# Cross-attention stage: side work moved between VectorE, GpSimd and the end of the stage

## The reference, cut to what matters

```python
cq = heads(ci @ cq_w, NH, CHD)            # 16 heads of 16
ckv = encoder_outputs @ ckv_w
ck, cv = jnp.split(ckv, 2, axis=-1)
cctx = sdpa(cq, ck, cv, causal=False)     # 512 queries x 1601 keys
cctx = cctx.transpose(0, 2, 1, 3).reshape(b, l, CC)      # CC = 256
hidden_states = hidden_states + cctx @ cdense_w          # 256 x 512
mi = rms_norm(hidden_states, ln_post_attn_w)
v_out = jax.nn.silu(mi @ v_gate) * (mi @ v_up) @ v_down
l_out = jax.nn.silu(mi @ l_gate) * (mi @ l_up) @ l_down
hidden_states = hidden_states + jnp.where(vm, v_out, l_out)
```

## Time and profile before

| | us |
|---|---|
| median of 3 runs | 2831.53 (2830.54 to 2838.45) |
| the profiled execution, device time | 2844.54 |
| its span | 2842.7 |
| PE busy | 2294.1 (81% of the span) |
| DVE busy | 1615.3 (57%) |
| ACT busy | 937.5 (33%) |
| POOL busy | 363.3 (13%) |

### The profile page before, as it was taken

One profiled execution on the slowest core, in us unless ns is written; L12 is line 12 of the kernel. 1 busy time (PEld: TensorE's weight loads), 2 busy tenths in 40 slices (PEclk: granted clock), 3 DMA queues, 4 the chain that ended last, 5 costly groups with the idle time before them and its releaser, 6 DMA issues. The chain is left out here.

```text
span 2842.7 us, 35384 instructions
## 1 busy us (share of the span) xinstructions
PE 2294.1 (81%) x13534; PEld 1463.7 (51%) x13534; DVE 1615.3 (57%) x2444; ACT 937.5 (33%) x1627; POOL 363.3 (13%) x388
## 2 busy tenths in 40 slices
PE   6987858869659867768687488999999859999968
PEld 3663545745446634546444333333333327877856
DVE  4384533664442854336554388788887626676534
ACT  1131132222121312312212237767777742222101
POOL 0120002110002200011100001111111112221211
PEclk8986879977779867889777669999999979999989
DMA  4033053250261240431412634433344013333322
GB/s 147 27 85 83 16 140 103 64 130 2 68 174 31 75 104 13 110 136 53 110 31 68 120 79 99 83 60 61 65 70 97 14 42 82 105 98 105 105 80 71
DMA packets 194542, 227.90 MB, mean 80 GB/s; under 512 B 53942, under 2 KB 128058, under 8 KB 193066
## 3 DMA queue, kind: packets, MB, share of 16 engines
q1 hardware_dynamic: 187404, 217.97, 31.1%
q0 software_dynamic: 6656, 6.96, 1.0%
q10 hardware_dynamic: 288, 0.27, 0.0%
HBM read 162.76 MB, written 34.98 MB: 70 GB/s over the span
## 5 line engine op out<-in xcount | busy, mean ns | idle before, releaser
L1435 DVE TENSOR_REDUCE quarters<-ps 128x2 f32<-128x804 f32 x512 | 484.4, 989 | 76.5 <-PE ps L1469 76.1
L1388 ACT ACTIVATE pT_x<-ps 128x512 f32<-128x512 f32 (+1 forms) x832 | 451.5, 594 | 166.6 <-PE ps L1497 144.7
L1469 PE MATMUL ps<-kx_ring,qx_ring 63*128 63x402 f32 x1024 | 235.5, 476 | 72.8 <-DVE quarters L1435 36.8
L184 DVE TENSOR_TENSOR w_lo<-w_raw,w_hi 128x512 fp32r<-128x512 f32 (+2 forms) x357 | 278.4, 780 | 12.2
L182 DVE CAST w_hi<-w_raw 128x512 fp32r<-128x512 f32 (+2 forms) x357 | 177.0, 496 | 185.2 <-PE ps L190 109.0
L1512 PE MATMUL ps<-pT_x,vx_ring 128*17 128x256 f32 (+1 forms) x3328 | 268.9, 397 | 0.0
L1469 PEld LDWEIGHTS ps<-kx_ring,qx_ring 63*128 63x128 f32 x1024 | 101.2, 197 | 268.9 <-DVE quarters L1435 162.8
L877 ACT ACTIVATE pT_s<-ps 128x1024 f32<-128x1024 f32 (+3 forms) x128 | 88.8, 704 | 355.7 <-PE ps L963 355.7
L188 PE MATMUL ps<-mi_h,w_hi 128*128 128x512 f32 (+1 forms) x440 | 174.6, 397 | 37.9 <-issue 25.7
L894 DVE TENSOR_REDUCE row_max_s<-ps 128x1 f32<-128x128 f32 (+3 forms) x256 | 123.8, 490 | 136.0 <-PE ps L933 132.1
L1497 PE MATMUL ps<-qx_ring,kx_ring 64*128 64x512 f32 (+1 forms) x832 | 181.6, 433 | 21.9 <-ACT pT_x L1388 18.4
(11 more groups left out here) (273 smaller groups left out, 4430.3 us busy)
## 6 DMA issues: line engine op xcount, KB each, us to landing
kx_ring<-cross_k_by_part SPq DMA_DIRECT2D x96, 200.2 KB, 7.3
w_raw<-L_xattn_l_qkv SPq DMA_DIRECT2D x48, 256.0 KB, 2.9
w_raw<-L_xattn_v_qkv SPq DMA_DIRECT2D x48, 256.0 KB, 2.7
w_raw<-L_xattn_l_gate SPq DMA_DIRECT2D x40, 256.0 KB, 2.9
w_raw<-L_xattn_l_up SPq DMA_DIRECT2D x40, 256.0 KB, 2.8
w_raw<-L_xattn_l_down SPq DMA_DIRECT2D x40, 256.0 KB, 2.7
q_st<-early SPq DMA_DIRECT2D x32, 256.0 KB, 5.2
cross_v_by_group<-v_aug SPq DMA_DIRECT2D x16, 442.0 KB
```

The lines of the kernel that those rows point to most:

```text
L184: nc.vector.tensor_tensor(out=lo, in0=raw, in1=hi.bitcast(f32), op=ALU.subtract).then_inc(s_split, 1)
L1388: nc.scalar.activation(pT[0:kn, u % 3, j, :], ps[0:kn, 5 + v % 3, :], ACT.Exp, scale=SCALE)\
L1435: nc.vector.tensor_reduce(out=quarters[:, g % 2, pair, :, q, quarter], in_=ps[:, at:at + 2, 0:MAXW], axis=AX.X, op=ALU.max)\
L1469: last = nc.tensor.matmul(ps[:, at + par, 0:MAXW], q_r[rows, g % RING, pair, q * P:(q + 1) * P], k_r[rows, g % RING, pair, k0:k0 + MAXW], ...
```

## The change

Seven edits, all in the cross attention but the last:

1. `flip` moves from `kt` 4 to `kt` 7 of the next group.
2. `back` (the scaling of the rows) and `low` (the low parts) leave DVE for POOL; `pack` now begins with the multiplication. On POOL, `shifts` stands ahead of `pack`.
3. `high` on ACT moves from `kt` 10 of even groups to `kt` 4 of odd groups, and `cross_h` and `cross_l` have 8 slots in place of 4.
4. The 12 `dense` units of batches 0 to 2 leave groups 5, 9 and 13 and stand behind the last group, after its `flip`, before the four of batch 3.
5. ACT's copy of the sums stands behind the third exponential of `kt` 1, not the second.
6. `h_all` is loaded in 16 pieces of 256 KB, one behind each group's loads, not in 4 of 1 MB.
7. `keep_all` is loaded at the start of the feed-forward, behind its first four weight tiles, with a wait on DVE (L1696) and POOL (L1647) there.

```diff
-                if g and kt == 4:
+                if g and kt == 7:
                     now.append(("flip", g - 1))
-                if g and kt == 8:
-                    now.append(("back", g - 1))
-                if g and g % 2 == 0 and kt == 11:
-                    now.append(("low", g // 2 - 1))
-                if g > 4 and g % 4 == 1 and kt % 3 == 0 and kt:
-                    now.append(("dense", g // 4 - 1, kt // 3 - 1))
...
-            by_step.append([("flip", g), ("back", g), ("low", g // 2)] + [("dense", g // 4, j) for j in range(4)])
+            early = [("dense", b, j) for b in range(groups // 4 - 1) for j in range(4)]
+            by_step.append([("flip", groups - 1)] + early + [("dense", groups // 4 - 1, j) for j in range(4)])
...
-                            if g - 2 < B:
-                                sp.dma_start(h_all[:, g - 2, :, :], h_d[g - 2]).then_inc(s["s_hin"], 16)
-                        for e in range(2):
-                            sp.dma_start(keep_all[:, e, :, :], keep_d[e:e + 1].broadcast_to((P, B, S))).then_inc(s["s_hin"], 16)
+                            sp.dma_start(h_all[:, (g - 2) // DT, (g - 2) % DT, :], h_d[(g - 2) // DT, :, (g - 2) % DT, :])\
+                                .then_inc(s["s_hin"], 16)
...
                         def pack(g):
+                            pool.wait_ge(s["s_rb"], 64 * (g + 1))
+                            if g:
+                                pool.wait_ge(s["s_ac"], 64 * g)
+                            nc.gpsimd.tensor_tensor(out=att[:, :], in0=osb[:, g % 2, :], in1=rq_rows[:, :], op=ALU.mult)\
+                                .then_inc(s["s_at"], 1)
...
+                        def low(n):
+                            pool.wait_ge(s["s_high"], n + 1)
+                            nc.gpsimd.tensor_tensor(out=al[:, n, :], in0=pairs[:, n % 2, :], in1=ah[:, n, :].bitcast(f32),
+                                                    op=ALU.subtract).then_inc(s["s_low"], 1)
...
                                 scale_rows(g - 1)
-                                pack(g - 1)
                             if g + 1 < NG:
                                 shifts(g + 1)
+                            if g:
+                                pack(g - 1)
+                            if g > 2 and g % 2:
+                                low(g // 2 - 1)
...
-                                if g and kt == 1 and j == 1:
+                                if g and kt == 1 and j == 2:
                                     keep_sums(g - 1)
-                            if g and g % 2 == 0 and kt == 10:
+                            if g > 2 and g % 2 and kt == 4:
                                 high(g // 2 - 1)
```

More of the change, by code:

```diff
@@ L1233, in cross_side_work, with cross_attention @@
                 by_step.append(now)
-            g = groups - 1
-            by_step.append([("flip", g), ("back", g), ("low", g // 2)] + [("dense", g // 4, j) for j in range(4)])
+            early = [("dense", b, j) for b in range(groups // 4 - 1) for j in range(4)]
+            by_step.append([("flip", groups - 1)] + early + [("dense", groups // 4 - 1, j) for j in range(4)])
             return start, by_step
-        def cross_attention(h_all, keep_all):
+        def cross_attention(h_all):
             RING, KQ_LOADS = 3, 12
@@ L1306, in _ @@
                             load_values(g)
-                            if g - 2 < B:
-                                sp.dma_start(h_all[:, g - 2, :, :], h_d[g - 2]).then_inc(s["s_hin"], 16)
-                        for e in range(2):
-                            sp.dma_start(keep_all[:, e, :, :], keep_d[e:e + 1].broadcast_to((P, B, S))).then_inc(s["s_hin"], 16)
-                        sp.wait_ge(s["s_hin"], 16 * (B + 2))
+                            sp.dma_start(h_all[:, (g - 2) // DT, (g - 2) % DT, :], h_d[(g - 2) // DT, :, (g - 2) % DT, :])\
+                                .then_inc(s["s_hin"], 16)
+                        for k in range(NG - 2, B * DT):
+                            sp.dma_start(h_all[:, k // DT, k % DT, :], h_d[k // DT, :, k % DT, :]).then_inc(s["s_hin"], 16)
+                        sp.wait_ge(s["s_hin"], 16 * B * DT)
                     @block.gpsimd
@@ L1354, in _ @@
                                 scale_rows(g - 1)
-                                pack(g - 1)
                             if g + 1 < NG:
                                 shifts(g + 1)
+                            if g:
+                                pack(g - 1)
+                            if g > 2 and g % 2:
+                                low(g // 2 - 1)
                         scale_rows(NG - 1)
                         pack(NG - 1)
+                        low(NG // 2 - 1)
                     @block.scalar
@@ L1372, in high @@
                             act.wait_ge(s["s_ac"], 128 * (n + 1))
-                            if n >= 4:
-                                act.wait_ge(s["s_used"], place["dense", n // 2 - 2, DT - 1] + 1)
-                            nc.scalar.activation(ah[:, n % 4, :], pairs[:, n % 2, :], ACT.Copy).then_inc(s["s_high"], 1)
+                            nc.scalar.activation(ah[:, n, :], pairs[:, n % 2, :], ACT.Copy).then_inc(s["s_high"], 1)
                         act.wait_ge(s["s_cw"], 16)
@@ L1408, in _ @@
                                                             op=ALU.subtract).then_inc(s["s_cl"], 1)
[L1409 to L1414, removed]
+                            if o[0] == "flip":
                                 g = o[1]
@@ L1419, in _ @@
                                 nc.vector.reciprocal(rq[:, :], sums[:, :]).then_inc(s["s_rq"], 1)
[L1420 to L1426, removed]
                             else:
@@ L1441, in _ @@
                                     b, j = o[1], o[2]
-                                    dve.wait_ge(s["s_hin"], 16 * B)
+                                    dve.wait_ge(s["s_hin"], 16 * B * DT)
                                     nc.vector.tensor_tensor(out=h_all[:, b, j, :], in0=h_all[:, b, j, :], in1=ps[:, at, :],
@@ L1480, in fill @@
                                 for k in range(ET):
-                                    last = three(ps[:, at, :], cdh[:, k, cols_j], cdl[:, k, cols_j], ah[:, (2 * b + k) % 4, :],
-                                                 al[:, (2 * b + k) % 4, :], k == 0, k == ET - 1)
+                                    last = three(ps[:, at, :], cdh[:, k, cols_j], cdl[:, k, cols_j], ah[:, 2 * b + k, :],
+                                                 al[:, 2 * b + k, :], k == 0, k == ET - 1)
                             last.then_inc(s["s_fill"], 1)
@@ L1592, in _ @@
                             load_w(sp, n, src, wl, s["s_ws"])
+                            if n == RAW - 1 and normed:
+                                for e in range(2):
+                                    sp.dma_start(keep_all[:, e, :, :], keep_d[e:e + 1].broadcast_to((P, B, S)))\
+                                        .then_inc(s["s_keep"], 16)
                             if w == "d" and c % NC == 4 and c > NC:
@@ L1646, in _ @@
                             pool.wait_ge(s["s_si"], c + 1)
+                            if c == 0 and normed:
+                                pool.wait_ge(s["s_keep"], 32)
                             nc.gpsimd.tensor_tensor(out=by_batch(sg[0:cn, c % 2, :]), in0=by_batch(sg[0:cn, c % 2, :]),
@@ L1694, in _ @@
                                     rest_x(0, k - 1)
+                            dve.wait_ge(s["s_keep"], 32)
                             for g in range(ST):
@@ L1796, in program @@
         h_all = sb("h_all", [P, B, DT, S])
+        cross_attention(h_all)
         keep_all = sb("keep_all", [P, 2, B, S])
-        cross_attention(h_all, keep_all)
         flags = sb("flags", [1, ST], i32)
```

4 lines of the change are left out of this document (2 added, 2 removed).

## The result

The changed kernel takes 2756.11 us (median of 4 runs, 2754.19 to 2762.2) against 2831.03 for the one before (2826.7 to 2838.45): a ratio of **0.9727** (95% interval 0.9708 to 0.9746), 74.9 us less. The prediction was 2755.0. Measured again on another occasion, the ratio was 0.972 (0.970 to 0.9741).

What follows compares the result with a forecast made beforehand. PE was taken to bound a group at 33.2 us without waits, taken as 34.0 against 39.99. Groups 1 to 13 -77.9, group 14 -1.0, group 15 +0.6, end +1.8: -76.5 from 2831.5 gives 2755.0 us, range 2744 to 2786.

Steps and rivals of the forecast that it cites:

- the copy: ACT's copy of the sums, one exponential later: worth 0 to 0.6 us a group, taken within the group's estimate.
- the rounding: ACT's `high` at step 4 of odd groups: 10.3 us of waits for packed pairs go, 0.6 of work stays.
- the clock: PE's granted clock in groups 1 to 13, below 1.00 with stalls: the rest of 77.9 us beyond the parts' 70.5.
- the inversion's step: DVE's `flip` at step 7, 4.5 us after the sums land: 23.7 us of DVE's waits go.
- the scaling and low parts: `back` and `low` moved to POOL: DVE loses 19 instructions in groups 1 to 13, 13.1 us.
- the projections: The 12 early `dense` units moved behind the last group: 1.95 us each, 23.4 us leave the groups.
- the order on POOL: Shift row ahead of packing's four issues, so the later inversion ahead of the shift was costed at nothing.
- The end: Last sums' DMA to last addition: 25.19 us before, 27.0 forecast, +1.8 (bounds -0.5 and +3.5).
- The feed-forward's start: `keep_all`, loaded there behind four weight tiles, lands near 2343 on the old time line: 0, other bound +2 us.
- GpSimd does not hold the reductions: Rival: GpSimd's moved operations hold DVE in the groups; groups of 36.6 us, about -42, 2789; chance 0.08.
- The waits did not move: Rival: sums land later, or PE and ACT hold each other; groups near 36.7 us, about -41, 2790; chance 0.07.
- The slower rival: Shift row late on POOL behind DVE's inversion, if sums land some 10 us later: +12 us, 2843; chance 0.03.

## Why the prediction was right

**What bounds.** Right. Without waits a group is PE's own work: 33.2 us by two spacings of PE's starts, 33.58 measured. I had taken 34.0 for the copy and the rounding; the copy's new place shows that it need not hold PE (0.47 us of the difference), and the rounding doesn't either: odd and even groups are alike.

**The parts.** The forecast for groups 1 to 13 was 77.9 us, of which the parts named 70.5 and the clock was to be the rest; 83.3 came. The terms did not hit. Undone alone, the inversion's step is worth 49.7 us in groups 1 to 13, not 23.7; the rounding's 52.1, not 10.3; the scaling and low parts 5.9, not 13.1; the projections 26.2 with group 14's, not 23.4; the copy 6.1; the order on POOL 107. These add up to far more than the 83.3 gained, so they are not shares of it: each is the price of one edit missing from the finished schedule. The estimate held since it was anchored on the bound of a group, not on the sum of its waits.

**Luck.** That the time came out 1.1 us from the forecast is in part luck. In the traces the change is worth 82.6 us (82.3 of device time), 6.1 more than forecast. The profiled execution of before lay 7.4 us further above its median than that of after, and this took the surplus back: 74.9 us between the medians. The second measurement had 2758.2 us, 77.8 less than the kernel before beside it.

**Where each went.** The inversion reached DVE 16.2 us after the sums' DMA, against 17.6 forecast, and the sums' second DMA was issued at 9.6, so there was room. The end: forecast 27.0, measured 27.08 in one profile and 25.36 in the other. The gap of PE was as told in both; the lower clock behind it, for which the 27.0 stood midway between none and a full start at the half clock, came in the first only, so that this hit is luck too. The feed-forward's start: DVE's look at `keep_all` (L1698) did not wait, and its idle time before `prod` was 5.31 us after 6.31.

**The rivals.** GpSimd does not hold the reductions: 0.992 us beside 1.29 us operations that never stretched, and the kernel with the operations on DVE was no faster in its groups. The Trainium skill (SBUF — State Buffer, Who interferes with whom) says that a reduction never contends with GpSimd on trn2, and this trace agrees. The waits did not move. The slower rival was real, though its trigger was misjudged: it takes not sums that land 10 us later, but one block of POOL's queue in the other order, 41.84 us a group and a ratio of 1.0071. The prediction gave the move of `shifts` no price of its own and used it only as the reason why a late inversion costs nothing; it is what the rest rests on.

## What to carry to other kernels

Bound a repeated unit by the spacing of the busiest engine's starts where nothing waits, and forecast a repair of waits from that bound, not from the sum of the waits: the same wait was 23.7 us here among others and 33.8 alone. When work is moved along an in-order queue, look at what small transfer stands behind it; one that a whole group waits for goes ahead of anything that can be late. The place of a step in a written order can have two bounds, with a different late transfer beyond each (here the sums and the shift row), so it is worth trying the places on both sides.

## What the hardware showed that I had not expected

A wait that reaches PE costs more than itself: 49.7 us for 33.8 of DVE's waits, 52.1 for 40.2 of ACT's, 107 for 63.2 of PE's. The granted clock falls with such waits, to 0.95, 0.95 and 0.87 as the means of the thirteen groups, where it is 1.00 without them, and PE's busy time for the same 4244 matmuls grows from 434.66 to 455.06, 447.52 and 479.15 us. The rest of each price is PE's idle time.

But the clock does not fall every time. At the end of the stage PE waits 2.91 us for DVE in one profile of the changed kernel and 2.73 in the other. In the first the stretch shows 0.94 (above), and two of the additions start 2.24 us apart; in the second

```profile
2212.30:2237.66 25.36, 21.90 (x93) 17.05 (x91) 11.03 (x17) 0.63 (x1) 8.27 (x13) 1.00 0.07 17
```

they start 1.40 us apart from the third on, and the same end is 27.08 - 25.36 = 1.7 us shorter. Group 14 shows the same without a long wait: it took 34.40 us at a clock of 1.00 in both profiles of the changed kernel, and 35.43 at 0.95 with the three projections put ahead of the last inversion, an edit that acts only behind group 15. What decides between the two stays open. So a difference of 1 to 2 us in one such stretch shows nothing of an edit until the clocks of both profiles are set side by side.
